# Splitting the first expert layer of batch 1 into a gating pass and a weighting pass

## The reference

```python
x = x + L0_xattn(layernorm(x), ctx, ctx, mask)     # 16 heads of 8, masked
x = x + L0_ffn(layernorm(x))                       # 16 experts of 96, 4 per token, and one shared expert
x = x + L1_xattn(layernorm(x), ctx, ctx)           # 16 heads of 8, its own layernorm inside
x = L1_ffn(x)                                      # 8 experts of 256, 2 per token, layernorms inside
```

```python
hact = jax.nn.silu(g) * u * combine[:, :, None]    # g = x w1, u = x w3, for all 16 experts
y = jnp.einsum('nei,ehi->nh', hact, w2)            # combine is 0 for experts that are not chosen
shared = jnp.einsum('ni,hi->nh', jax.nn.silu(x @ ws1.T) * (x @ ws3.T), ws2)
```

## Time and profile before

| | |
|---|---|
| median of three runs | 299.78 us (297.86 to 302.04) |
| profiled execution, device time | 295.13 us |
| its span | 293.2 us |
| mean granted TensorE clock | 0.941 of full |
| PE busy | 247.4 us (84%) |
| DVE busy | 201.1 us (69%) |
| ACT busy | 149.8 us (51%) |
| POOL busy | 82.0 us (28%) |

### The profile page before, as it was taken

The page is one execution under the profiler, slowest core; times in us unless marked ns, Lnnn a source line. Parts: engine busy times, 40 slices in busy tenths (PEclk is TensorE's granted clock), DMA queues, the critical chain, the costliest instruction groups (busy, mean ns, idle before and its releaser), DMA issues.

```text
span 293.2 us, 5209 instructions
## 1 busy us (share of the span) xinstructions
PE 247.4 (84%) x1701; PEld 141.3 (48%) x1712; DVE 201.1 (69%) x603; ACT 149.8 (51%) x218; POOL 82.0 (28%) x225
## 2 busy tenths in 40 slices
PE   3937989899977996788898898999998889898970
PEld 1611444454443573666576434444444346555670
DVE  5828767766755844597866985767676538888854
ACT  6710466557744743441322454677666535727360
POOL 8504564265522000100300341222213103433321
PEclk9985799999999998999999857999999999999997
DMA  7388597701100068600032630500000000000000
GB/s 235 134 237 180 114 192 273 185 1 57 56 1 0 2 102 128 95 0 0 0 96 69 198 90 0 161 3 1 2 2 0 1 2 1 0 2 0 19 2 18
DMA packets 18406, 19.52 MB, mean 67 GB/s; under 512 B 1996, under 2 KB 16180, under 8 KB 18036
## 3 DMA queue, kind: packets, MB, share of 16 engines
q1 hardware_dynamic: 17804, 18.25, 25.5%
q10 hardware_dynamic: 576, 0.94, 0.9%
HBM read 14.98 MB, written 4.19 MB: 65 GB/s over the span
## 4 chain that ended last, share of the span: by engine, by line
PE 60%; DVE 20%; issue 8%; DMA 5%; ACT 3%; SPq 1%; POOL 1%; DVEq 1%; POOLq 0%; ACTq 0%
PE bank L410 11%; PE bank L342 8%; PE bank L387 8%; PE bank L533 5%; PE bank L564 5%; DVE row_max L794 4%; PE bank L356 4%; PE bank L383 3%; DMA k_stack<-k_bounce 3%; PE bank L498 2%; PE bank L515 2%; PE bank L499 2%; PE bank L549 2%; PE bank L535 2%; DVE early L943 2%
## 5 line engine op out<-in xcount | busy, mean ns | idle before, releaser
L1247 ACT ACTIVATE probs<-bank 128x1024 f32<-128x1024 f32 x64 | 65.4, 1024 | 33.2 <-PE bank L387 28.1
L342 PE MATMUL bank<-k_stack,q_stack 72*128 72x512 bf16 x128 | 53.7, 425 | 10.4 <-DMA q_stack<-q_bounce 4.4
L791 DVE CUSTOM_DVE_ANT_0 discard<-bank,bias_q 128x512 bf16<-128x512 f32 x64 | 42.6, 689 | 26.4 <-PE bank L342 23.6
L387 PE MATMUL bank<-q_stack,k_stack 99*128 99x256 bf16 x256 | 51.6, 287 | 1.3 <-issue 1.0
L794 DVE TENSOR_REDUCE row_max<-bank 128x1 f32<-128x512 f32 x64 | 40.9, 684 | 14.0 <-PE bank L342 13.3
L1233 ACT COPY q_stack<-bank 3x512 bf16<-3x512 bf16 x32 | 18.5, 578 | 36.4 <-PE bank L356 35.7
L410 PE MATMUL bank<-probs,v_ext 128*32 128x256 f32 x512 | 35.1, 393 | 0.8 <-ACT o_sb L1254 0.8
L387 PEld LDWEIGHTS bank<-q_stack,k_stack 99*128 99x128 bf16 x256 | 24.7, 102 | 22.1 <-issue 4.7
L1459 POOL CAST max_part<-row_max 128x4 bf16<-128x4 f32 x32 | 6.6, 207 | 93.1 <-DVE row_max L794 57.2
L342 PEld LDWEIGHTS bank<-k_stack,q_stack 72*128 72x128 bf16 x128 | 12.7, 101 | 33.3 <-DVE row_max L794 9.6
L1329 ACT ACTIVATE early<-bank,col 128x256 f32<-128x256 f32 x32 | 15.5, 563 | 18.7 <-PE bank L549 18.7
(11 more groups left out here) (179 smaller groups left out, 380.2 us busy)
## 6 DMA issues: line engine op xcount, KB each, us to landing
k_stack<-k_bounce SPq DMA_DIRECT2D x9, 384.0 KB
q_bounce<-q_part SPq DMA_DIRECT2D x12, 192.0 KB, 2.4
q_stack<-q_bounce SPq DMA_DIRECT2D x3, 576.0 KB
k_bounce<-early SPq DMA_DIRECT2D x4, 384.0 KB, 2.6
experts_w<-in_wu SPq DMA_DIRECT2D x1, 1024.0 KB, 5.1
experts_w<-in_wg SPq DMA_DIRECT2D x1, 816.0 KB, 9.4
experts_w<-in_wu SPq DMA_DIRECT2D x1, 816.0 KB, 10.9
experts_w<-in_wd SPq DMA_DIRECT2D x1, 768.0 KB, 7.2
```

Source lines behind the costliest of these rows:

```text
L342: mm(bank[:, qt, :], q_stack[0:STACK, b, h, qt * 128:(qt + 1) * 128], k_stack[0:STACK, b, h, :], start=True, stop=True).then_inc(for_max, 1)
L387: last = mm(o, k_stack[:, b, h, kt * 128:(kt + 1) * 128], q_stack[:, b, h, :], start=(l == 1), stop=(l == 1 or kt == kts[-1]))
L791: ins = dve.tensor_tensor_reduce(discard[:, qt, :], bank[:, qt, :], bias_q[:, qt, :], 1.0, LOWEST, ALU.add, ALU.max, o)
L1247: act.activation(probs[:, n % (2 * HG), :], bank[:, at:at + 2, :].rearrange("p a n -> p (a n)"), ACT.Exp, scale=SCALE).then_inc(exp_done, 1)
```

## The change

The units of batch 1 are split into two phases. `gate_late(i)` makes only silu(g) * u, into a buffer of its own per unit, `gated_late`, which lies in `probs`; `combine_late(i)` later multiplies it by the spread weights into `hid0`. The shared unit is multiplied down straight from `gated_late`. Banks and silu slots of batch 1's later units are released by the first phase (semaphore `gated_done`), no longer by `hid0_ready`. Batch 0's last routing part, its weight transpose, copy, first spread, first silu and first hidden unit move into the steps 34 to 40 of the first attention, and the order of the calls between the attentions is written anew on PE, DVE and ACT.

```diff
+        gated_late = probs.rearrange("p a n -> p (a n)")[:, 0:PAIRS0 * 2 * S].rearrange("p (i j s) -> p i j s", i=PAIRS0, j=2)
...
-            return (4, 2)[i % 2], PAIRS0 + i - 2 if i >= 2 else 4 + i
+            return (4, 2)[i % 2], -1 if i >= 2 else 4 + i
...                                    # PE, score_cols
                     if n == HEADS:
-                        pe.wait_ge(hid0_ready, B * PAIRS0)
+                        pe.wait_ge(hid0_ready, B * PAIRS0 - 1)
+                        pe.wait_ge(gated_done, PAIRS0)
...                                    # PE, up0
+                if b == 1 and i >= 2:
+                    pe.wait_ge(gated_done, i - 1)
...                                    # PE, down0
-                pe.wait_ge(hid0_ready, u + 1)
+                hidden = gated_late[:, i] if b == 1 and shared else hid0[:, u % 2]
+                if b == 1 and shared:
+                    pe.wait_ge(gated_done, PAIRS0)
+                else:
+                    pe.wait_ge(hid0_ready, u + 1)
...                                    # PE, extra list of the first attention
+                (37, lambda: combine_transpose(0, 0)),
+                (38, lambda: spread0(0, 0)),
...                                    # PE, between the attentions
             up0(0, 1)
             o_transpose(B * NG - 1)
+            spread0(0, 1)
             up0(0, 2)
-            combine_transpose(0, 0)
-            spread0(0, 0)
-            spread0(0, 1)
             att_transpose(0, 1)
+            down0(0, 0)
             spread0(0, 2)
-            down0(0, 0)
             out_projection(0, 1)
+            up0(0, 3)
             down0(0, 1)
             spread0(0, 3)
-            up0(0, 3)
+            up0(0, 4)
             transpose_tokens("f0", 1)
+            down0(0, 2)
+            spread0(0, 4)
             gate_logits(0, 1)
...
             down0(0, 5)
-            up0(1, 0)
+            up0(1, 1)
+            down0(0, 6)
+            up0(1, 2)
+            up0(1, 3)
             combine_transpose(0, 1)
-            down0(0, 6)
+            up0(1, 4)
             spread0(1, 0)
-            up0(1, 1)
+            transpose_tokens("a1n", 0)
+            up0(1, 5)
+            q_projection(1, 0)
             spread0(1, 1)
+            up0(1, 6)
             down0(1, 0)
             spread0(1, 2)
-            up0(1, 2)
-            transpose_tokens("a1n", 0)
-            q_projection(1, 0)
             down0(1, 1)
...                                    # DVE
+            def gate_late(i):
+                u = PAIRS0 + i
+                at, _ = banks0(1, i)
+                dve.wait_ge(silu_done, u + 1)
+                if i == 0:
+                    dve.wait_ge(pv_done, B * NG)
+                m, n = (I0, 1) if i == T0 // 2 else (128, 2)
+                tt(gated_late[0:m, i, 0:n], silu_g[0:m, u % 2, 0:n], bank[0:m, at:at + n, S:2 * S], ALU.mult)\
+                    .then_inc(gated_done, 1)
+
+            def combine_late(i):
+                u = PAIRS0 + i
+                dve.wait_ge(gated_done, i + 1)
+                dve.wait_ge(down0_done, u - 1)
+                dve.wait_ge(c_spread, T0 // 2 + i + 1)
+                tt(hid0[:, u % 2], gated_late[:, i], c_sb[:, u % 2], ALU.mult).then_inc(hid0_ready, 1)
...                                    # DVE, extra list of the first attention
-                (39, lambda: route0(0, 3)),
+                (34, lambda: route0(0, 3)),
+                (38, lambda: c_copy(0, 0)),
+                (40, lambda: hidden0(0)),
...                                    # DVE, between the attentions: the new order in full
             divide(B * NG - 1)
+            hidden0(1)
             attT_copy(0, 1)
+            hidden0(2)
             add_attention(0, 1)
+            hidden0(3)
             normalise("f0", 1, res[1][1])
             xT_copy("f0", 1)
+            hidden0(4)
             route0(1, 0)
+            hidden0(5)
             route0(1, 1)
+            hidden0(6)
+            gate_late(0)
             route0(1, 2)
+            gate_late(1)
+            add_experts0(0)
             route0(1, 3)
             c_copy(0, 1)
+            gate_late(2)
             normalise("a1", 0, res[2][0])
             norm_stats("a1n", 0, norm["a1"][0])
+            gate_late(3)
             normalise("a1n", 0, norm["a1"][0])
+            gate_late(4)
+            combine_late(0)
             xT_copy("a1n", 0)
+            gate_late(5)
             q_split(1, 0)
+            combine_late(1)
+            gate_late(6)
+            combine_late(2)
+            combine_late(3)
+            combine_late(4)
             head_max(HEADS + 0, 0)
             head_max(HEADS + 0, 1)
+            combine_late(5)
             head_max(HEADS + 1, 0)
...                                    # ACT, silu
-                if u >= 2:
+                if u >= 2 and u < PAIRS0 + 2:
                     act.wait_ge(hid0_ready, u - 1)
+                if u >= PAIRS0 + 2:
+                    act.wait_ge(gated_done, i - 1)
...                                    # ACT, extra list of the first attention
+                (38, lambda: first_silu()),
+                (39, lambda: c_evacuate(0, 0)),
...                                    # ACT, between the attentions
+            silu(0, 1)
             c_evacuate(0, 1)
-            silu(0, 1)
+            silu(0, 2)
             c_evacuate(0, 2)
+            silu(0, 3)
             c_evacuate(0, 3)
-            silu(0, 2)
-            silu(0, 3)
-            gate_exponential(0, 1)
             silu(0, 4)
             c_evacuate(0, 4)
+            gate_exponential(0, 1)
+            load_table(2, ACT.Silu)
             silu(0, 5)
-            load_table(2, ACT.Silu)
             c_evacuate(0, 5)
             silu(0, 6)
             silu(1, 0)
-            c_evacuate(1, 0)
             silu(1, 1)
...
+            c_evacuate(1, 0)
+            silu(1, 5)
+            c_evacuate(1, 1)
+            silu(1, 6)
+            c_evacuate(1, 2)
...
```

More of the change, by code:

```diff
@@ L255, in attention_ffn_kernel @@
         hid0_ready = sem("hid0_ready")
+        gated_done = sem("gated_done")
         down0_done = sem("down0_done")
@@ L514, in down0 @@
                     for t in range(QT):
-                        last = mm(bank[:, OUT, t * D:(t + 1) * D], hid0[0:m, u % 2, j, t * 128:(t + 1) * 128], w,
+                        last = mm(bank[:, OUT, t * D:(t + 1) * D], hidden[0:m, j, t * 128:(t + 1) * 128], w,
                                   start=(i == 0 and j == 0 and t == 0), stop=shared, skip_group_check=True)
@@ L662, in _ @@
             score_rows(HEADS + 1, 0)
-            up0(1, 6)
             score_rows(HEADS + 1, 1)
@@ L930, in route1, with hidden0 @@
                     .then_inc(combined[1], 1)
-            def hidden0(b, i):
-                u = b * PAIRS0 + i
-                at, _ = banks0(b, i)
-                dve.wait_ge(silu_done, u + 1)
-                if u >= 2:
-                    dve.wait_ge(down0_done, u - 1)
+            def hidden0(i):
+                at, _ = banks0(0, i)
+                dve.wait_ge(silu_done, i + 1)
+                if i >= 2:
+                    dve.wait_ge(down0_done, i - 1)
                 if i == T0 // 2:
-                    tt(hid0[0:I0, u % 2, 0, :], silu_g[0:I0, u % 2, 0, :], bank[0:I0, at, S:2 * S], ALU.mult)\
+                    tt(hid0[0:I0, i % 2, 0, :], silu_g[0:I0, i % 2, 0, :], bank[0:I0, at, S:2 * S], ALU.mult)\
                         .then_inc(hid0_ready, 1)
                     return
-                then(tt(gated[:, u % 2], silu_g[:, u % 2], bank[:, at:at + 2, S:2 * S], ALU.mult))
-                dve.wait_ge(c_spread, b * (T0 // 2) + i + 1)
-                tt(hid0[:, u % 2], gated[:, u % 2], c_sb[:, u % 2], ALU.mult).then_inc(hid0_ready, 1)
+                then(tt(gated[:, i % 2], silu_g[:, i % 2], bank[:, at:at + 2, S:2 * S], ALU.mult))
+                dve.wait_ge(c_spread, i + 1)
+                tt(hid0[:, i % 2], gated[:, i % 2], c_sb[:, i % 2], ALU.mult).then_inc(hid0_ready, 1)
+            def gate_late(i):
[13 more added lines that the diff above has]
+                tt(hid0[:, u % 2], gated_late[:, i], c_sb[:, u % 2], ALU.mult).then_inc(hid0_ready, 1)
             def add_experts0(b):
@@ L1331, in gelu1, with first_silu @@
                                        scale=col[:, COL_G1 + c:COL_G1 + c + 1]).then_inc(gelu_done, 1)
+            def first_silu():
+                for i in range(4):
+                    act.wait_ge(k_written[i], 16)
+                silu(0, 0)
             attention(0, [
@@ L1336, in _ @@
                 (37, lambda: load_table(1, ACT.Silu)),
-            ])
-            for i in range(4):
-                act.wait_ge(k_written[i], 16)
-            silu(0, 0)
-            c_evacuate(0, 0)
+                (38, lambda: first_silu()),
+                (39, lambda: c_evacuate(0, 0)),
+            ])
+            silu(0, 1)
             c_evacuate(0, 1)
-            silu(0, 1)
+            silu(0, 2)
```

(16 more changed lines are left out.)

29 lines of the change are left out of this document (4 added, 25 removed).

## The result

The changed kernel took 305.4 us (median of four runs, 304.61 to 307.59), the kernel before 300.91 us beside it. The ratio is 1.0265, with a 95% interval of 1.0212 to 1.0318: some 8 us slower. I had forecast 300.3 us and given "slower by over 2%" a chance of 0.07. Ratios here leave out executions well above the fastest of the same kernel (one of e8's took 1261.21 us), so they differ from quotients of medians, and the profiles of e2, e4 and e8 are of such executions, late already at the last exponential of the first attention (109.61, 111.33 and 111.21 us). That matters for the size of the loss: the two medians above lie only 4.5 us apart, 1.5 per cent. The changed kernel was therefore measured again (e12), six times beside 23 executions of the kernel before: medians of 306.46 and 298.89 us, ratio 1.0275. So the loss is real, and 8 us is about its size.

What follows compares the result with a forecast made beforehand. It took a chain of waits through both attentions on PE and DVE as the bound. Terms -1.5, +1.8, +0.45, -3.05, +2.2, +1.3, -0.7 gave +0.5 us on 299.78: 300.3 us, range 295.5 to 304.5.

Steps and rivals of the forecast that it cites:

- Part 1: End of the first attention: at full clock, add_attention(0, 1) starts at 117.2 instead of 118.69, -1.5 us.
- My upper bound of 0: End of the first attention: no gain at add_attention(0, 1) if the clock falls all the same.
- Parts 2 and 3: From add_attention to batch 1's routing (+1.8 and +0.45 us), then to add_experts0(0) (-3.05 us).
- part 3: From batch 1's routing to add_experts0(0): reached at 136.5 instead of 138.84, a term of -3.05 us.
- Part 4: From add_experts0(0) to batch 0's tokens: moved routing gives the gain back, +2.2 us; normalise a1 at 141.2.
- Part 5: Up to the q split: late gating products and up0(1, 5) stand before it, +1.3 us; q split 1.2 us later.
- The rival of the slower side: Clock falls before the second attention's scores, +1.4 us: 301.7, or 304 if the slow stretch lasts; chance 0.25.
- Part 6: First scores of the second attention: DVE, free when they come, absorbs 0.7 of 1.2 us; +0.5 us stays.

Runs made afterwards that it cites:

- e8: Two phases with add_experts0(0) and batch 0's chain placed ahead of batch 1's last routing part, plus 13 small unused matmuls; 0.9935 of the kernel before.
- e12: The changed kernel measured again, unaltered, beside the kernel before; ratio 1.0275, median 306.46 us.
- e14: The changed kernel plus seven unused matmuls in PE's routing waits and 13 small ones among the second attention's first scores; 1.0006 of the kernel before.
- e2: The changed kernel plus seven unused matmuls on PE where it waited for the routing; ratio 1.0148 to the kernel before.
- e4: The kernel before with only batch 0's earlier weights and new unit order, batch 1 in one phase; ratio 1.0125 to the kernel before.
- e6: Two phases, batch 0 as before, add_experts0(0) and its chain ahead of batch 1's last routing part, first scores before the last two spreads; 1.0060 of the kernel before.
- e7: The kernel before plus 13 small unused matmuls between the first scores of the second attention; ratio 0.9935 to the kernel before.

## Why the prediction was wrong

**Part 1 failed first.** I took the end of the first attention at full clock, "PE is now kept busier". PE waited 0.62 and 0.81 us for MISC, up0(0, 1) followed at half speed, 110.77 to 114.2, 3.45 us for 1.83, and add_attention was 0.4 late instead of 1.5 early. My upper bound of 0 said the clock might fall "all the same"; I let it into neither sum nor range. e14 has the same two waits, 0.62 and 0.81, yet its clock stayed up, and there the milestone is 14.41: -1.25. So the order did what I had said, the clock did not, and the two waits alone do not decide whether it falls.

**Parts 2 and 3 held** as intervals: from add_attention to the routing 8.96 us against 8.65 forecast, from there to add_experts0(0) 10.82 against 10.65. The step of part 3 itself, -3.05 forecast, was -2.93. That add_experts0(0) still came no sooner than before is the error of part 1, 1.9 us, and 0.5 from parts 2 and 3 against the 2.3 forecast.

**Part 4** was 0.6 short at normalise a1: 5.32 for 4.7. One operand cast of the routing took 0.71 us where its neighbours took 0.19, beside POOL's addition (DVE, then POOL):

```profile
142.92 0.71 DVE L900 CAST c_part<-combine 128x32 bf16<-128x32 f32 x1
```

```profile
142.86 0.72 POOL L1454 TENSOR_TENSOR res_bias<-res,row 128x256 f32<-128x256 f32 x1
```

The first normalise pair took 0.59 instead of 1.01. So the 0.4 moved to the routing, as I had worked out from the rule of the Trainium skill ("SBUF — State Buffer", "SBUF: two separate sides") that DVE and GpSimd exclude each other at a shared port pair. The trace agrees, with 0.5.

**Part 5 is the step that cost most.** Its waits were the right ones, in the right order: DVE ahead of the last gating product, up0(1, 5) ahead of q_projection. But I had them from normalise a1n to the q split at 4.1 us and they took 8.2. The term that failed is the price of an up product, 1.83 us: up0(1, 4) and up0(1, 5) took 3.7 and 3.4 us (145.94 to 149.65, 151.58 to 154.99), at half clock, after PE had been idle for 3.0 of the 3.3 us ahead of the first. That idle time follows from part 4's own order: routing part 3 stands between add_experts0(0) and the gating product whose bank up0(1, 4) needs. I did not ask what it would trigger. e2 fills it, and with the clock held the same way takes 4.41 us, 0.3 from my 4.1: the waits were right, the clock was what failed.

**The rival of the slower side** had the right mechanism and the wrong place and price. I looked for PE's idle time behind the last spread, 155.7 to 159.1, and priced row maxima at 0.2 a head. The clock fell ahead of the chain at 145.1, with two up products next in PE's order, and also at about 110.9, 158.7, 169.0 and 179.2. The rule of the Trainium skill ("TensorE: Matmul & The Clock Gate", "What's actually happening"), that the slow clock is the default and activity releases it, I weighed with 0.25 and for one place only. By it every stretch where the change makes PE wait was to be asked about. The trace agrees at 145.1, but not every sparse stretch ends in a fall: in the kernel before, PE was busy for 0.54 us from 122 to 124 and 0.95 from 134 to 136, and the clock stayed at 1.00.

**Part 6** had 0.7 us absorbed by DVE; here the maximum of HEADS + 2 began 4.71 us behind the scores (forecast 3.65, before 4.38). DVE waited 0.22 and 0.90 us for score products, which stand behind down products at half clock (DVE timeline of the changed kernel, the first maxima, as the earlier trace rows):

```profile
168.63 1.29 DVE L803 TENSOR_REDUCE row_max<-bank 128x1 f32<-128x512 f32 x2 [2.29 <-PE bank L344]
169.84 0.68 DVE L970 TENSOR_TENSOR early<-probs,early 128x512 f32<-128x512 f32 x1
170.74 1.29 DVE L803 TENSOR_REDUCE row_max<-bank 128x1 f32<-128x512 f32 x2 [0.22 <-PE bank L344]
172.93 4.30 DVE L803 TENSOR_REDUCE row_max<-bank 128x1 f32<-128x512 f32 x7 [0.90 <-PE bank L344]
```

From its first DMA to the scores the changed kernel took 9.77 us (8.82 before). SP spent 2.33 us on the three issues that took 1.47 before; in e12, the same kernel, they took 1.47 again and the scores came after 8.90 (the SP rows, changed and e12):

```profile
158.45 2.33 SPq L1622 DMA_DIRECT2D q_bounce<-q_part  x3
```

```profile
160.50 1.47 SPq L1622 DMA_DIRECT2D q_bounce<-q_part  x3
```

So this 1.0 us is of one execution and not of the change. So is most of what the first maxima lost: in e12 that of HEADS + 2 began 3.77 us behind the scores, close to the forecast 3.65, and the rest of the kernel took 135.0 us, as before (135.3). Part 6 held there.

With the clock held up by padding, e14 ends 0.5 us behind the unpadded kernel before, my very number, but with q split +2.4 where I had +1.2: that agreement is chance.

## What to carry to other kernels

When an edit makes TensorE wait for another engine, price the clock too: list every stretch in which the new schedule leaves it idle, and double the duration of what follows if that lies on the way to a DMA or a serial chain. Splitting work into two phases costs most where a phase stands in front of the chain that another stage waits for; placed behind that chain (e6), the two phases were still 0.6 per cent slower than one phase, and padded (e8) as fast. Where TensorE's light work lets the clock fall, a few products that compute nothing can be worth more than a reordering.

## What the runs showed of the hardware

In the first steps of the second attention PE was busy for 10.29 of 11 us at a clock of 0.51; with 13 products of 128 columns more (e7) it was busy for 9.26 of 11 at 1.00, and the kernel was faster, by 0.65 and 1.0 per cent in two measurements. A high busy share in the profile thus does not mean that the clock is held: at half the clock the same light work only looks fuller.
